# A graph network over a 4096 x 4096 adjacency: first three block rows side by side by columns, two parameter arrays, slots free longest

## The reference

```python
def layer0(x):                       # "gcn"
    return relu((adj @ x) @ kernel + bias)
def mlp(x, W1, b1, W2, b2, W3, b3):  # leaky_relu after each of three 128x128 layers
    ...
def layer1(u):                       # three rounds
    for _ in range(3):
        v = mlp(adj @ u, *uv)
        u = mlp(adj @ v, *vu)
    return v
x = layernorm(x + layer0(x))
x = layernorm(x + layer1(x))
```

## Time and profile before

| | us |
|---|---|
| median of 3 runs | 1195.95 |
| lowest, highest | 1193.66, 1197.58 |
| the profiled execution, whole | 1194.43 |
| its span in the profile | 1192.7 |

### The profile page before, as it was taken

One profiled execution on the slowest core, in us unless ns is written; L12 is line 12 of the kernel. 1 busy time (PEld: TensorE's weight loads), 2 busy tenths in 40 slices (PEclk: granted clock), 3 DMA queues, 4 the chain that ended last, 5 costly groups with the idle time before them and its releaser, 6 DMA issues.

```text
span 1192.7 us, 13593 instructions
## 1 busy us (share of the span) xinstructions
PE 1164.0 (98%) x5200; PEld 950.8 (80%) x5200; DVE 733.8 (62%) x888; ACT 643.9 (54%) x771; POOL 0.2 (0%) x4
## 2 busy tenths in 40 slices
PE   7889999999999999999999999999999999999996
PEld 5678888887888887788888788888778888877874
DVE  7878765467465545565545646644565554658996
ACT  7756553346555544565445646543556444557672
POOL 0000000000000000000000000000000000000000
PEclk9899999999999999999999999999999999999998
DMA  9878766565355555655547635655564656569881
GB/s 366 321 280 311 266 232 227 205 247 202 152 199 208 185 184 203 220 170 201 194 177 246 214 138 178 214 193 182 193 243 156 211 184 226 179 250 344 290 315 69
DMA packets 74656, 261.60 MB, mean 219 GB/s; under 512 B 8800, under 2 KB 10080, under 8 KB 74592
## 3 DMA queue, kind: packets, MB, share of 16 engines
q1 hardware_dynamic: 74592, 260.74, 62.1%
HBM read 258.61 MB, written 2.10 MB: 219 GB/s over the span
## 4 chain that ended last, share of the span: by engine, by line
PE 87%; DVE 6%; DMA 5%; ACT 1%; issue 1%; SPq 0%; DVEq 0%; ACTq 0%
PE agg_ps L599 26%; PE agg_ps L600 26%; PE agg_ps L601 26%; DMA adj_raw<-in_adj 5%; DVE adj_lo L591 3%; PE pre_ps L631 3%; ACT adj_hi L491 1%; PE hid_ps L599 1%; PE hid_ps L601 1%; PE hid_ps L600 1%; PE hid_ps L643 1%; PE hid_ps L660 1%; DVE resid L515 1%; DVE stats L501 1%; PE hid_ps L657 0%
## 5 line engine op out<-in xcount | busy, mean ns | idle before, releaser
L591 DVE TENSOR_TENSOR adj_lo<-adj_raw,adj_hi 128x1024 fp32r<-128x1024 f32 x488 | 577.2, 1220 | 307.6 <-ACT adj_hi L491 303.3
L599 PE MATMUL agg_ps<-adj_hi,feat_hi 128*128 128x512 f32 x1536 | 617.0, 402 | 8.8 <-DVE adj_lo L591 8.8
L600 PE MATMUL agg_ps<-adj_lo,feat_hi 128*128 128x512 f32 x1536 | 600.5, 391 | 0.0
L601 PE MATMUL agg_ps<-adj_hi,feat_lo 128*128 128x512 f32 x1536 | 600.1, 391 | 0.0
L491 ACT ACTIVATE adj_hi<-adj_raw 128x1024 fp32r<-128x1024 f32 x488 | 491.9, 1051 | 93.7 <-DMA adj_raw<-in_adj 85.3
L599 PEld LDWEIGHTS agg_ps<-adj_hi,feat_hi 128*128 128x128 f32 x1536 | 290.0, 189 | 76.5 <-issue 14.8
L600 PEld LDWEIGHTS agg_ps<-adj_lo,feat_hi 128*128 128x128 f32 x1536 | 289.8, 189 | 65.0 <-issue 7.0
L601 PEld LDWEIGHTS agg_ps<-adj_hi,feat_lo 128*128 128x128 f32 x1536 | 289.4, 188 | 61.5
L403 ACT ACTIVATE hid<-hid_ps,b_col 128x512 f32<-128x512 f32 x80 | 54.7, 684 | 71.9 <-PE hid_ps L601 57.6
L403 ACT ACTIVATE post<-pre 128x512 f32<-128x512 f32 x40 | 25.2, 630 | 93.0 <-DVE pre L562 91.5
L458 ACT ACTIVATE in_hi<-part 128x512 fp32r<-128x512 f32 x24 | 15.2, 635 | 106.3 <-DVE part L581 106.3
(11 more groups left out here) (39 smaller groups left out, 230.0 us busy)
## 6 DMA issues: line engine op xcount, KB each, us to landing
adj_raw<-in_adj SPq DMA_DIRECT2D x488, 512.0 KB, 5.6
resid<-in_x SPq DMA_DIRECT2D x8, 256.0 KB, 7.6
out<-resid SPq DMA_DIRECT2D x8, 256.0 KB, 4.0
w_raw<-in_uv_W SPq DMA_DIRECT2D x3, 64.0 KB, 2.6
w_raw<-in_vu_W SPq DMA_DIRECT2D x3, 64.0 KB, 2.3
w_raw<-in_gcn_w SPq DMA_DIRECT2D x1, 64.0 KB, 6.1
b_row<-in_gcn_b SPq DMA_DIRECT2D x1, 64.0 KB, 6.3
b_row<-in_uv_b SPq DMA_DIRECT2D x1, 64.0 KB, 3.8
```

Of the source, the lines that this page charges most:

```text
L591: dve.tensor_tensor(adj_lo[:, b % RING, slot], adj_raw[:, h % RAW, 0:pieces * CHUNK], adj_hi[:, b % RING, slot].bitcast(F32), ALU.subtract ...
L599: pe.matmul(to, l_hi, r_hi, start=start, stop=False)
L600: pe.matmul(to, l_hi, r_lo, start=False, stop=False)
L601: return pe.matmul(to, l_lo, r_hi, start=False, stop=stop)
```

## The change

- Sweep 0 starts with rows 0, 1 and 2 side by side: for columns 7 down to 3 the three blocks of a column come one after the other, in three PSUM banks. Then the remaining corner is written out (`FIRST_CORNER`), so that rows 0, 1 and 2 close at block uses 20, 22 and 23, and four blocks of row 3 and three `begin` uses follow. From block use 32 on the order is as before.
- An x chunk is loaded with the first block that needs it (`brings_x`), which is now every third block.
- The halves of blocks whose first use is one of the first 24 stand 4 ticks ahead of it in ACT's and DVE's programs (`FIRST_LEAD`), where it was 12. All other halves keep 12.
- The 14 parameter DMAs become two: one array of 128 x 900 (all matrices and bias columns, 0.461 MB) and one of three bias rows (0.197 MB into 128 partitions), both issued before half 46. `pe_out` of unit 0 waits for both.
- A block takes the slot whose last block ends first by the order, instead of slot b mod 5.

```diff
-FIRST_PARAMS, OTHER_PARAMS = 18, 34
+SIDE_BY_SIDE = 3
+FIRST_CORNER = (("finish", 0, (2,)), ("finish", 1, (2,)), ("finish", 2, (2,)), ("finish", 0, (1,)), ("finish", 1, (1,)), ("finish", 0, (0,)), ("finish", 2, (1,)), ("finish", 1, (0,)), ("finish", 2, (0,)), ("finish", 3, (7, 6, 5)), ("begin", 1, (0,)), ("begin", 2, (0,)), ("finish", 3, (4,)), ("begin", 2, (1,)), ("finish", 3, (3,)), ("both", 3, (0, 1, 2)))
+LEAD, FIRST_LEAD, FIRST_ROWS = 12, 4, 3
+LOAD_PARAMS = 46
...
-            yield from finish(s, 0, range(rows))
-            for r in range(1, top):
+            for c in range(top, SIDE_BY_SIDE - 1, -1):
+                for r in range(SIDE_BY_SIDE):
+                    yield s, FINISH, r, c
+            for what, r, columns in FIRST_CORNER:
+                yield from dict(finish=finish, begin=begin, both=both)[what](s, r, columns)
+            for r in range(SIDE_BY_SIDE + 1, top):
...
+        self.slot, self.before, holder = [], [], [None] * RING
+        for b in range(len(self.blocks)):
+            k = min(range(RING), key=lambda k: -1 if holder[k] is None else self.ends[holder[k]])
+            self.slot.append(k)
+            self.before.append(holder[k])
+            holder[k] = b
...
-            free = 0 if b < RING else self.ends[b - RING] * TILES + i + pieces
-            self.due.append(max(free, first * TILES + i - LEAD))
+            free = 0 if self.before[b] is None else self.ends[self.before[b]] * TILES + i + pieces
+            lead = FIRST_LEAD if first < FIRST_ROWS * rows else LEAD
+            self.due.append(max(free, first * TILES + i - lead))
...
-                if h == FIRST_PARAMS:
-                    load_weight(OUT_W[GCN], gcn_params_loaded)
-                    load_bias_row(OUT_BIAS[GCN], gcn_params_loaded)
-                if h == OTHER_PARAMS:
...
+                if h == LOAD_PARAMS:
+                    sp.dma_start(params[:, :], weights).then_inc(params_loaded, 16)
+                    sp.dma_start(b_row[:, :], bias_rows.partition_broadcast(P)).then_inc(params_loaded, 16)
...
-                        pe.wait_ge(gcn_params_loaded, 16 * N_GCN_PARAMS)
+                        pe.wait_ge(params_loaded, 32)
```

More of the change, by code:

```diff
@@ L134, in __init__ @@
             self.bank.append(g)
+        self.brings_x = {}
+        for b, (s, r, c) in enumerate(blocks):
+            if s == 0 and c not in self.brings_x.values():
+                self.brings_x[b] = c
+        self.xs = list(self.brings_x.values())
         self.blocks = [(self.node(s, r), self.node(s, c)) for s, r, c in blocks]
@@ L310, in gnn_kernel @@
         out_written = sem("out_written")
+        w_raw = params[:, 0:N_WEIGHTS * P].rearrange("p (n f) -> p n f", f=P)
+        b_col = params[:, N_WEIGHTS * P:]
         kind_of = plan.kind_of
@@ L483, in _ @@
                     b, i, pieces = plan.loads[h]
-                    if b < C and i == 0:
-                        act.wait_ge(x_loaded[b], 16)
-                        act.activation(feat_hi[0][:, columns(b)], resid[:, columns(b)], ACT.Copy)\
+                    if b in plan.brings_x and i == 0:
+                        c = plan.brings_x[b]
+                        act.wait_ge(x_loaded[c], 16)
+                        act.activation(feat_hi[0][:, columns(c)], resid[:, columns(c)], ACT.Copy)\
                            .then_inc(x_hi_ready, 1)
                     act.wait_ge(adj_loaded[h % RAW], 16 * (h // RAW + 1))
-                    if b >= RING:
-                        act.wait_ge(half_used, 2 * plan.ends[b - RING] + (i + pieces + 1) // 2)
-                    act.activation(adj_hi[:, b % RING, i * CHUNK:(i + pieces) * CHUNK],
+                    if plan.before[b] is not None:
+                        act.wait_ge(half_used, 2 * plan.ends[plan.before[b]] + (i + pieces + 1) // 2)
+                    act.activation(adj_hi[:, plan.slot[b], i * CHUNK:(i + pieces) * CHUNK],
                                    adj_raw[:, h % RAW, 0:pieces * CHUNK], ACT.Copy).then_inc(adj_hi_ready, 1)
@@ L562, in _ @@
                     dve.tensor_tensor(by_tile(pre[:, own(u)]), by_tile(pre_ps[:, own(u)]),
-                                      b_row[:, b:b + 1, :].to_broadcast([P, len(tiles_of(u)), P]), ALU.add)\
+                                      b_row[:, b * P:(b + 1) * P].rearrange("p (j f) -> p j f", f=P)
+                                      .to_broadcast([P, len(tiles_of(u)), P]), ALU.add)\
                        .then_inc(pre_ready, 1)
@@ L713 @@
     out = nc.dram_tensor("out", arrays["x"].shape, F32, kind="ExternalOutput").ap()
-    uv, vu = ({part: aps[f"{tag}_{part}"] for part in ("W1", "b1", "W2", "b2", "W3", "b3")} for tag in ("uv", "vu"))
-    gnn_kernel(nc, aps["x"], aps["adj"], aps["gcn_w"], aps["gcn_b"], uv, vu, out)
+    gnn_kernel(nc, aps["x"], aps["adj"], aps["weights"], aps["bias_rows"], out)
     ran = _run(nc, [{f"in_{name}": a for name, a in arrays.items()}], core_ids=[0])
```

66 lines of the change are left out of this document (24 added, 42 removed).

## The result

| | median us | lowest to highest | profiled execution | its span |
|---|---|---|---|---|
| before | 1195.95 | 1193.66 to 1197.58 | 1194.43 | 1192.7 |
| after | 1187.27 | 1186.32 to 1187.81 | 1187.08 | 1185.3 |

The medians are of five executions before and four after. The ratio of the runs is 0.9927, with a 95% interval of 0.9912 to 0.9942: 8.7 us faster, where 8.0 were forecast. In the two profiled executions the difference is 7.4 us, because the one of the kernel before was 1.5 us faster than its median.

What follows compares the result with a forecast made beforehand. PE bounds the kernel, with gain only before unit 2's `pe_out`: after waits of 0.85 and 2.4 and a clock fall of 1.6 it starts at 91.0 instead of 98.97, 8.0 us less, so 1188.0 us, range 1184.0 to 1193.0.

Steps and rivals of the forecast that it cites:

- What bounds the kernel: PE's start: all gain lies before unit 2's `pe_out` at 98.97 us; two holes there cost 6.9 and 5.2.
- Transfers: Row 0 to 2 blocks: arrivals ruled by bytes at about 406 GB/s, no PE hole expected up to tick 84, 68.5 us.
- Parameters: Ahead of unit 0's `pe_out`: the two arrays land at 71.4, PE stands from 70.55, a wait of 0.85, bounds 0 and 2.
- Half 47 and 48: After unit 0's `pe_out`: DVE has half 47 split at 77.2, PE needs it at 77.06, tick 94, 0.15 late.
- Unit 1: Its ACT copy behind half 51 (79.4), table load and root ends at 81.7; 2.4 us of idle PE, bounds 0.8 and 3.4.
- The drain: At unit 1's table load: a skill rule's extra 1.38 us would make the gain 1.4 smaller; none was charged.
- Clock: After unit 1's wait of 2.4 us the clock falls, charged 1.6, bounds 0 and 2.1.
- Unit 2: At tick 106: DVE's half 53 done at 89.7, PE wants it at 90.3, just in time; `pe_out` at 91.0.
- Slots: Slot choice from half 56 on: nothing charged; without cover it could at most save some tenths.
- Rival (a): Long start stretch: rate only 380 GB/s, half 51 4.7 us later, gain 3.3, time 1192.6; chance 0.17.
- Rival (c): First three `pe_out`: each meets a 6.9 us hole behind split bursts on ACT; 8.5 us slower, 1204; chance 0.04.
- Rival (d): Later sweeps: order or slots bring a wait that eats the gain, within 3 us of before; chance 0.04.

Runs made afterwards that it cites:

- a_table: Changed kernel with one more instruction, a square root at the start of ACT's program that loads the root's table early; 1186.41 us, ratio 0.9917.
- c_two: Changed kernel with layer 0's parameters alone first and the root's table loaded at the start; 1185.64 us, ratio 0.9915.
- b_slots: Kernel before with the longest-free slots alone; order, lead and parameters as before; 1196.10 us, ratio 1.0001.
- b_params: Kernel before with the two parameter arrays alone, both issued before half 18; 1190.90 us, ratio 0.9956.
- a_order: Changed kernel's order and slots, with lead 12 throughout and fourteen parameter DMAs at the old places into the packed arrays; 1191.88 us, ratio 0.9967.
- a_gcnfirst: Changed kernel with layer 0's two parameters before half 44 and the rest in three DMAs before half 56; 1184.97 us, ratio 0.9907.
- c_three: Changed kernel with layer 0's parameters first, the table loaded at the start, and 12 ticks between the first three chains; 1189.24 us, ratio 0.9947.
- a_params14: Changed kernel with fourteen parameter DMAs instead of two, all before half 46; 1188.27 us, ratio 0.9937.
- a_spacing: Changed kernel with 12 ticks instead of 10 between the chains of units 0, 1 and 2; 1189.14 us, ratio 0.9946.
- a_lead12: Changed kernel with a lead of 12 ticks for all halves; 1188.90 us, ratio 0.9938.

## Why the prediction was right, point by point

- **What bounds the kernel.** Right in the main: the old start held the gain, and the stretch behind the third `pe_out` is the same to 0.1 us. That it is the same so exactly is luck: 1 us was won over the middle sweeps and 1 lost in the last, and the forecast had neither.
- **Transfers.** The mechanism held: 404 to 407 GB/s from 30 to 60 us. The claim of no hole up to tick 84 was not exact. PE started at 7.29 and not at 8.55, and left the slow spacing of 0.43 us after 7 matmuls and not after 14, so that the 15th came at 11.90 and not at 14.56. It reached tick 87 at 70.47 against a reckoned 70.55: about 2.5 us went into small waits such as the 0.82 at 35.93. Starting earlier bought nothing, since the bytes came at their own pace.
- **Parameters.** The wait was 1.66 between modelled ends, 1.8 by starts, against 0.85. The landing time was right (7.7 us for the bias rows, 6.3 + 1.3 forecast); half 39 was 0.7 later than my rule, so the issues were.
- **Half 47 and 48.** DVE was 0.8 us late (78.91) where I had 0.15.
- **Unit 1.** Half 51 left ACT at 80.92, 1.5 later than 79.4: the rule was early by the 1 us that the old trace had shown, and by a little more. The copy ended at 83.01 against 81.7. The idle time ahead of this `pe_out` was 1.81 and not 2 to 3, because PE too was late.
- **The drain.** "ScalarE: Activation LUTs", section "What ACT_TABLE_LOAD costs", in the Trainium skill puts 1.38 us beside a table load. Here again the root starts at 82.23, 0.01 us after the load; taking the load away moved the second `pe_out` by 2.0, of which 0.6 came from the first one. No run here shows a drain.
- **Clock.** Charged with 1.6, cost 0: it did not fall. This made up for what was too small before it, the second `pe_out` being 1.4 late (83.06 against 81.7). The total, 7.3 against 8.0 in the profiles, is better than its parts, and that is luck. (A slip in its working: the first old hole begins at 36.18, so a fall at 38.3 is 2.1 us into it and not 2.3.)
- **Unit 2.** That DVE's half 53 stands right behind was right (90.78, forecast 89.7), and a_table shows it to be what decides: the distance from half 47 to the third `pe_out` is 13.98 to 13.99 us in the changed kernel, in a_table and in c_two, with a hole of 1.81, 0.42 or none ahead of the second `pe_out`.
- **Slots.** Right: nothing (b_slots, in the old order).
- **Rival (a)**, a lower rate over the long stretch: fell. "HBM Reference", section "Specifications (TRN2)", in the Trainium skill gives 358 GB/s as a core's share beside a remark that a core alone gets more; this core alone held 404 to 407 over three windows in a row, so the share was not the limit.
- **Rival (c)**: its mechanism, a copy behind splits, is there once with 1.8 us, and 5.4 with a lead of 12.
- **Rival (d)**, a wait in later sweeps: there is one, of 1.32 us at 1142.46 (0.28 before), far too small to eat the gain.

What the prediction did not price is how the parts share the gain. By medians, alone in the old kernel the arrays are worth 5.0, the order with its slots 4.1, the lead 2.7 and the slots 0: 11.8 together, against 8.7 for the whole. About 1 us of this is in two of the numbers, since b_params and a_order both have the packed arrays. For the rest, each fills the same idle time up to what the byte stream and DVE's chain allow. So taking one back costs little: 1.6 for the lead, 0.9 for the fourteen DMAs, by medians, and neither is clear of the intervals. That DVE's chain is a limit is shown by a_table. That the byte stream is the other is argued from the rate of 404 to 407 GB/s, and a_gcnfirst fits it: with 0.53 MB taken out of the stretch, DVE had half 47 1.9 us earlier.

## What to carry to other kernels

Pick an instruction that has the same work behind it in both kernels, at the place where the bound engine is fed at last, and compare its start; the rest of the trace then is a check that nothing is given back, at several places, since two changes of 1 us can cancel in the sum. In an in-order engine look for the instruction that others wait for and count what stands ahead of it: a stock of loads taken early makes it late while transfers are the bound, and a stock too small lets the next wait through to the DMA queue. Small DMAs of parameters belong outside the stretch in which the queue is full, in few pieces, and those that are needed early go alone.

## What the runs showed of the hardware

- The clock's fall goes not by the length of a hole alone. The granted clock fell to 0.50 in or soon after holes of 1.88 (c_three), 2.02 (a_gcnfirst), 2.08 (a_params14), 3.21 (c_three) and 3.23 us (a_spacing). It stayed at 1.00 after holes of 1.81 (after), 2.61 (a_params14) and 3.15 (a_order, 1.00 from 80 to 88). The holes of 3.4 us and more (before, b_slots, b_params, a_lead12, a_order) all brought a fall. What decides between 1.9 and 3.2 us stays open.
- The matmuls right behind a hole don't tell whether the clock falls. In a_spacing the `pe_out` after the hole took 1.16 us at full clock, and the fall came at 86.0, when PE had been busy again for 1.3 us; in the kernel before it came at 38.3, some 2.1 us into the hole. The clock column of narrow windows shows both.
- The first half's split on ACT starts at 4.78 to 5.03 us in the kernels with the new order and at 5.41 to 6.09 in the four with the old one, though it is issued as the second DMA at 1.17 us in both before and after. In the old order an x chunk stands fourth in the queue, in the new one a half. Why a later DMA changes an earlier one's landing was not tried.
